# A twelve-layer perceiver kernel: batches of the head-wise cross attention reordered, one mask product in place of two, and layers begun on three quarters of their tokens

## The reference

```python
def cross(q_in, ctx, mask):                     # layer 4; layer 10 has no mask and one shared k and v head
    q, k, v = heads(q_in @ Wq + bq), heads(ctx @ Wk + bk), heads(ctx @ Wv + bv)
    s = where(mask, q @ k.T / sqrt(8), -1e9)    # 64 x 16 x 32 x 257
    return merge(softmax(s) @ v) @ Wo + bo
x = x + cross(layernorm(x), ctx, mask)
```

## Time and profile before

| | us |
|---|---|
| median of three runs | 3074.31 (3073.43 to 3076.48) |
| the profiled execution, own time | 3070.85 |
| its span | 3069.1 |
| mean granted TensorE clock | 0.95 of full |

### The profile page before, as it was taken

How to read it: one execution, slowest core, us unless ns; L and a number is a source line. 1 busy time by engine, 2 the same in 40 slices (tenths; PEclk the granted TensorE clock), 3 DMA queues, 4 the chain that set the end, 5 groups by cost and what they waited for, 6 DMA issues and landing times.

```text
span 3069.1 us, 71179 instructions
## 1 busy us (share of the span) xinstructions
PE 2812.5 (92%) x27569; PEld 1813.6 (59%) x27569; DVE 1702.2 (55%) x5653; ACT 1319.7 (43%) x3579; POOL 689.9 (22%) x1524
## 2 busy tenths in 40 slices
PE   8999998997999978999689997779999999999898
PEld 7888885554567755665457775534444444444465
DVE  6777777674166677558746765842233232232544
ACT  4655555542278842348538883411111121121222
POOL 2444440000067720024116661100000000000000
PEclk9999999998999988888779998989999999999999
DMA  5111110000021100230011113040000000000000
GB/s 133 49 47 47 49 31 8 2 3 5 12 55 48 48 25 3 67 106 2 5 40 43 39 29 142 2 136 1 1 1 1 1 1 1 1 1 1 1 1 14
DMA packets 125910, 92.28 MB, mean 30 GB/s; under 512 B 41027, under 2 KB 122566, under 8 KB 124230
## 3 DMA queue, kind: packets, MB, share of 16 engines
q1 hardware_dynamic: 125574, 87.74, 10.1%
HBM read 84.02 MB, written 3.67 MB: 29 GB/s over the span
## 4 chain that ended last, share of the span: by engine, by line
PE 54%; DVE 7%; issue 5%; POOL 4%; ACT 3%; DVEq 2%; POOLq 2%; ACTq 0%
PE banks L3349 24%; POOL probs L1208 3%; PE banks L918 2%; PE banks L3768 2%; PE banks L3759 2%; PE banks L3757 2%; PE banks L1682 2%; PE banks L899 1%; POOLq L1209 1%; PE banks L927 1%; PE banks L886 1%; PE banks L3404 1%; PE banks L2301 1%; PE banks L3359 1%; PE banks L1924 1%
## 5 line engine op out<-in xcount | busy, mean ns | idle before, releaser
L1008 ACT ACTIVATE probs<-probs,nbias 128x257 f32<-128x257 f32 x512 | 254.7, 507 | 0.0
L1208 POOL TENSOR_SCALAR probs<-probs,rinv 128x257 f32<-128x257 f32 x512 | 237.9, 485 | 29.3 <-DVE rinv L1102 25.6
L3349 PE MATMUL banks<-Wz,hT 128*64 128x256 f32 x2048 | 226.4, 379 | 0.0
L3349 PE MATMUL banks<-Wn,hT 128*64 128x512 f32 x1024 | 225.4, 593 | 0.0
L3349 PE MATMUL banks<-Wr,hT 128*64 128x512 f32 x1024 | 225.2, 592 | 0.0
L3618 POOL COPY rb<-hT 128x512 f32<-128x512 f32 x32 | 35.8, 1119 | 801.3 <-ACT hT L3424 777.0
L3349 PEld LDWEIGHTS banks<-Wz,hT 128*64 128x64 f32 x2048 | 147.0, 137 | 87.7 <-issue 18.3
L3592 DVE TENSOR_TENSOR pr<-hb,banks 128x512 f32<-128x512 f32 x32 | 22.0, 688 | 298.3 <-PE banks L3404 298.3
L712 POOL TENSOR_SCALAR probs<-probs,rinv 128x257 f32<-128x257 f32 x256 | 120.6, 485 | 201.3 <-DVE rinv L652 200.7
L3349 PEld LDWEIGHTS banks<-Wr,hT 128*64 128x64 f32 x1024 | 73.5, 137 | 132.6 <-issue 128.0
L3349 PEld LDWEIGHTS banks<-Wn,hT 128*64 128x64 f32 x1024 | 70.9, 137 | 129.5 <-issue 129.5
(11 more groups left out here) (632 smaller groups left out, 6399.2 us busy)
## 6 DMA issues: line engine op xcount, KB each, us to landing
kvT<-in_ctx_T SPq DMA_DIRECT2D x192, 128.5 KB
kv<-in_ctx SPq DMA_DIRECT2D x64, 128.0 KB
kv<-in_ctx SPq DMA_DIRECT2D x32, 256.0 KB
W<-in_L_ffn_W_T SPq DMA_DIRECT2D x2, 2048.0 KB
Wr<-in_L_ffn_w_hh_T SPq DMA_DIRECT2D x1, 4096.0 KB
Wn<-in_L_ffn_w_hh_T SPq DMA_DIRECT2D x1, 4096.0 KB
Wz<-in_L_ffn_w_hh_T SPq DMA_DIRECT2D x1, 4096.0 KB
v_last<-v_last SPq DMA_DIRECT2D x192, 8.0 KB, 1.6
```

The costliest lines, as they stand in the source:

```text
L1008: i = e.activation(s, s, ACT.Exp, bias=self.nbias[v][:, r:r + 1], scale=self.scale, accum_out=self.rows_sum[v][:, r:r + 1])
L1208: e.tensor_scalar(s, s, self.rinv[v][:, r:r + 1], 1.0, ALU.mult, ALU.mult)
L3349: mm = e.matmul(self.bank[b][hf * BATCH:(hf + 1) * BATCH, 0:n], lhs, rhs, start=start, stop=stop, tile_position=(0, hf * BATCH))
```

## The change

1. In layers 4 and 10 keys and values are made six batches ahead instead of five, on TensorE behind the scores instead of ahead of them, with a ring of seven value tiles instead of six. ScalarE makes the exponentials of g+3 ahead of the copies of keys and values. GpSimd's put_k_last moves along.
2. In layer 4 one product with the mask stays: it adds -BIG to masked scores (sink), and the row maxima's instruction multiplies by a factor (1 for seen places, a small number for masked ones that brings -BIG to the masked value) where it added a fill.
3. Nine layer starts (2, 3, 4 and 6 to 11) are reordered: norm_pe and norm_act_yT take a list of quarters, the layer's first products wait only for the quarters that they read, and quarter 3 is transposed a little later inside the layer. Where banks 0 to 3 are in use by then, the transposes go to others (TURN_BANKS). In layer 3 VectorE makes the signs ahead of the norm.

```diff
+    TURN_BANKS = (0, 1, 2, 3)
...
     def norm_dve(self, e):
-
-        quarters = range(3 if self.index else 0, 4)
+        self.norm_dve_statistics(e)
+        self.norm_dve_rows(e)
+
+    def own_quarters(self):
+        return range(3 if self.index else 0, 4)
+
+    def norm_dve_statistics(self, e):
         self.prog.x_loaded.wait_ge(e, 1)
-        for q in quarters:
+        for q in self.own_quarters():
...
-    X_BANK, T_BANK, AV, RING, PROBS, V_RING = 4, 5, 7, 4, 5, 6
+    X_BANK, T_BANK, AV, RING, PROBS, V_RING = 4, 5, 7, 4, 5, 7
...
-        p.constants_made.wait_ge(e, 1)
+        self.norm_pe(e, (0,))
...
+        self.norm_pe(e, (1, 2))
+        self.x_free = None
+        self.n_yT.wait_ge(e, 1)
+        self.prep_act.wait_ge(e, 1)
+        self.project(e, 0)
         self.prep_act.wait_ge(e, 3)
         e.matmul(bank[7][:, 0:P], p.ones[0:1, :], self.bo_eff[:, :], start=True, stop=True).then_inc(self.prep_mm.up(), 1)
-        self.norm_pe(e)
-        self.x_free = None
+        self.keys_values(e, 0)
+        self.norm_pe(e, (3,))
         self.n_yT.wait_ge(e, 4)
-        self.project(e, 0)
-        self.keys_values(e, 0)
         self.prep_act.wait_ge(e, 4)
         self.prep_pool.wait_ge(e, 1)
-        for g in range(1, 5):
+        for g in range(1, 6):
             self.keys_values(e, g)
+            if g == 5:
+                break
...
-            if g + 5 < BATCH:
-                self.keys_values(e, g + 5)
             if g + 4 < BATCH:
                 self.scores(e, g + 4)
+            if g + 6 < BATCH:
+                self.keys_values(e, g + 6)
             if b == 3 and t + 2 < NT:
                 self.project(e, t + 2)
             if b == 1 and t:
...
-            for n in range(2):
-                for r in range(4):
-                    rows = slice(32 * r, 32 * r + 32)
-                    i = e.matmul(self.bank[r][:, 0:CTX], self.tiled_ident[n][rows, :], self.lift[t % 2][rows, b * CTX:(b + 1) * CTX],
-                                 start=False, stop=n == 1)
-                    if n:
-                        i.then_inc(self.scored.up(), 1)
+            for r in range(4):
+                rows = slice(32 * r, 32 * r + 32)
+                e.matmul(self.bank[r][:, 0:CTX], self.tiled_ident[rows, :], self.sink[t % 2][rows, b * CTX:(b + 1) * CTX],
+                         start=False, stop=True).then_inc(self.scored.up(), 1)
...
+        self.copy_keys_values(e, 5)
         self.copy_pT1(e, 0)
         for g in range(BATCH):
-            if g + 5 < BATCH:
-                self.copy_keys_values(e, g + 5)
             if g + 3 < BATCH:
                 self.exponentials(e, g + 3)
+            if g + 6 < BATCH:
+                self.copy_keys_values(e, g + 6)
...
-        self.norm_dve(e)
+        self.norm_dve_statistics(e)
         self.weights_wait(e)
         self.take_queries(e, 0)
+        self.norm_dve_rows(e)
...
-            add = self.fill[t % 2][:, b * CTX:(b + 1) * CTX]
+            with_mask, op = self.factor[t % 2][:, b * CTX:(b + 1) * CTX], ALU.mult
         else:
-            add = self.zeros[:, :]
+            with_mask, op = self.zeros[:, :], ALU.add
...
-            i = e.tensor_tensor_reduce(self.probs[v][:, r * CTX:(r + 1) * CTX], self.bank[r][:, 0:CTX], add, 1.0, -3.0e38, ALU.add, ALU.max,
+            i = e.tensor_tensor_reduce(self.probs[v][:, r * CTX:(r + 1) * CTX], self.bank[r][:, 0:CTX], with_mask, 1.0, -3.0e38, op, ALU.max,
...
-        self.prog.rowed.wait_ge(e, NT * (self.index + 1))
-        self.map_lift(e, 0)
-        self.map_fill(e, 0)
+        self.map_sink(e, 0)
+        self.map_factor(e, 0)
...
-            if g + 5 < BATCH:
-                self.put_k_last(e, g + 5)
+            if g + 6 < BATCH:
+                self.put_k_last(e, g + 6)
...
-        e.tensor_scalar(self.lift[t % 2][:, :], self.mask_u8[:, :], -self.BIG, self.BIG, ALU.mult, ALU.add)
-
-    def map_fill(self, e, t):
+        e.tensor_scalar(self.sink[t % 2][:, :], self.mask_u8[:, :], self.BIG, -self.BIG, ALU.mult, ALU.add)
...
-        e.tensor_scalar(self.fill[t % 2][:, :], self.mask_u8[:, :], -to, to, ALU.mult, ALU.add)
+        e.tensor_scalar(self.factor[t % 2][:, :], self.mask_u8[:, :], 1.0 - f, f, ALU.mult, ALU.add)
...
-        self.norm_pe(e)
+        self.norm_pe(e, (0, 1, 2))
         self.weights_wait(e)
         for c in range(self.C):
             self.features(e, 0, c)
+            if c == 1:
+                self.norm_pe(e, (3,))
...
-            self.n_yT.wait_ge(e, 4)
+            self.n_yT.wait_ge(e, r + t + 1 if r == 0 else 4)
...
+        self.norm_act_yT(e, (0, 1))
         self.norm_act_std(e)
-        self.norm_act_yT(e)
+        self.norm_act_yT(e, (2,))
...
-        self.norm_pe(e)
+        self.norm_pe(e, (0, 1, 2))
...
+            if r == 2:
+                self.norm_pe(e, (3,))
             for c in range(FC):
+                self.n_yT.wait_ge(e, max(r, c % 2) + 1)
                 self.relu0.wait_ge(e, FC * r + c - 1)
...
+            self.signs_ready.wait_ge(e, 3)
+            self.n_yT.wait_ge(e, 3)
...
+        self.weights_wait(e)
         FC = self.FC
         for r in range(self.ROUNDS):
             h0, h1 = self.h[r % 2]
+            if r == 1:
+                self.norm_act_std(e)
+            if r == 2:
+                self.signs_ready.wait_ge(e, 3)
+                self.norm_act_yT(e, (3,))
             self.mm2.wait_ge(e, r - 1)
             for c in range(FC):
                 self.mm0.wait_ge(e, FC * r + c + 1)
...
                         self.next_root(e, q)
 
     def dve(self, e):
+        self.weights_wait(e)
+        e.tensor_scalar(self.W[0][:, :], self.raw[0][:, :], 2.0, -1.0, ALU.mult, ALU.add)
+        e.drain()
+        e.tensor_tensor(self.W[0][:, 0:512], self.W[0][:, 0:512], self.W[0][:, 512:1024], ALU.subtract).then_inc(self.signs_ready.up(), 1)
+        e.tensor_scalar(self.scales[:, 1:3], self.scales[:, 1:3], 2.0, None, ALU.mult).then_inc(self.signs_ready.up(), 1)
+        for n in range(1, 3):
+            e.tensor_scalar(self.W[n][:, :], self.raw[n][:, :], 2.0, -1.0, ALU.mult, ALU.add)
+        e.drain().then_inc(self.signs_ready.up(), 1)
         self.norm_dve(e)
-        self.weights_wait(e)
-        for n in range(3):
-            e.tensor_scalar(self.W[n][:, :], self.raw[n][:, :], 2.0, -1.0, ALU.mult, ALU.add)
-        e.tensor_scalar(self.scales[:, 1:3], self.scales[:, 1:3], 2.0, None, ALU.mult)
-        e.drain()
-        e.tensor_tensor(self.W[0][:, 0:512], self.W[0][:, 0:512], self.W[0][:, 512:1024], ALU.subtract)
-        e.drain().then_inc(self.signs_ready.up(), 1)
```

122 lines of the change are left out of this document (76 added, 46 removed).

## The result

The changed kernel takes 3195.81 us (median of four runs, 3189.34 to 3201.5); the kernel before, on the same chip, 3073.87. The ratio is 1.0398 with a 95% interval of 1.0374 to 1.0421: slower by 122 us. The forecast was 3197. The profiled execution took 3196.2 us, its span is 3194.5.

The account below looks back on a forecast made before the run. TensorE, busy 92% and without slack in layers 4 and 10, with ScalarE nearly full, was taken as the bound; 141 (loop) - 1 (mask product) - 17 (layer starts) = +123 us gave 3197 us, range 3155 to 3250.

Parts of the forecast that it names:

- The loop: Layers 4 and 10: TensorE's second user of bank 4 waits for ScalarE's delayed v copy; +141 us, bounds 122 to 170.
- The term for b = 0: In the round's iteration without a second user of bank 4, VectorE's late row maxima delay the next scores: +0.3 us.
- The upper bound of the loop: 85 us a layer in layers 4 and 10, with the raw 3.59 us and VectorE late in every iteration; 170 together.
- rival (d): Copies and stall are real, but TensorE catches up in b = 0 and layer starts gain their upper bound: 3160, chance 0.06.
- exponentials before the copies: Heading for layers 4 and 10: ScalarE's four exponentials now precede the kT and v copies; priced at +141 us together.
- TensorE has no slack: Layer 4's steady round: TensorE busy 15.43 of 15.48 us, so a new wait on it shows in the time at once.
- The mask product: Layer 4: four of eight bf16 matmuls per batch go, mostly hidden in waits; 1 us gained, bounds 0 and 4.
- The layer starts: Nine layers begin on three quarters: layer 2 gains 2.5 us, layer 3 3.5, others 11; 17 together, bounds 6 and 26.
- What would show it: Signs named: rounds of 20 to 21.5 us, 41 waits for v a layer of 1.3 to 1.9 us, clock near 1.00.
- (a): VectorE joins the loop in layers 4 and 10: exponentials wait 0.2 to 0.3 us more for nbias; 3225, chance 0.13.
- (b): TensorE's clock falls because it idles more, 7.4 us a round over half the 28 rounds: 3300, chance 0.09.
- (c): Faster: TensorE does not meet the wait for v, and rounds fall to about 14.4 us: 3026, chance 0.04.

Follow-up runs that it names:

- old-loops kernel: The changed kernel with both loop orders of layers 4 and 10 as before, five batches ahead; single mask product and new layer starts stay: 3056.74 us, ratio 0.9947.

## Why the prediction was right, and where it was not

**The loop (141 us).** Right in mechanism and size. From the start of one pT copy to the next, steady round of layer 4:

| iteration | before | forecast | measured |
|---|---|---|---|
| b = 0 | 3.3 | 3.6 | 3.81 |
| b = 1 | 3.54 | 5.25 | 5.22 |
| b = 2 | 4.66 | 6.3 | 6.22 |
| b = 3 | 3.96 | 5.5 | 5.47 |
| round | 15.48 | 20.7 | 20.72 |

Over the 64 batches, first pT copy to last, layer 4 took 238.8 us before and 310.1 now (+71.3; forecast 71), layer 10 234.8 and 303.8 (+69.0; forecast 70). The waits for v are 40 in layer 4 (41 named), in the weight loads 1.69, 1.28 and 1.25 us (1.3 to 1.9 named).

**The term for b = 0** was undersized, 0.3 for 0.5 us a round. The cause it names, VectorE's late row maxima, is what the rows show: the scores come 0.12 us behind the last maximum, while the spread queries had been ready for 0.36 us. In the sum that is 3 us a layer too little, and the terms for b = 1 to 3 a little too large make up for it.

**Readings.** The prediction takes the 0.24 us in the rows of the kernel before for a wait for v. The weight load behind the mask product comes 0.21 us late there also where it has nobody to wait for (L927 in b = 0), so only some 0.03 us of it was a wait for v, and L936's 0.31 us ends with GpSimd's p_last. The upper bound of the loop, 85 us a layer, does not hold both things that it names: with the raw 3.59 us (41 times 0.29 more) and VectorE late in every iteration (14 more) the sum is 97. And the 3160 of rival (d) has no working. None of these entered the forecast itself.

**What the sum left implicit.** It treats the 141 us as the price of "exponentials before the copies". The runs show that either order alone costs (scores first 109, exponentials first 161), so undoing the exponentials' edit gives back only 34 us. The sum was right because it followed all of TensorE's and ScalarE's order round the loop once; its heading, "exponentials before the copies", would have misled anyone who mended the kernel by it. Nor does "TensorE has no slack" say what bounded the kernel before: taking 0.3 us of TensorE's work out of a round left it at 15.47.

**The mask product** (1 us, 0 to 4): the round of the changed kernel shows 0.1, or 1.4 us in layer 4; the timed difference of 3 us has an interval wider than itself. The reason given, that it falls into the wait for ScalarE, is what the rows show (1.28 against 1.17).

**The layer starts** (17 us, 6 to 26) were oversized, and the two that the prediction works out, layers 2 and 3, both came out otherwise. The old-loops kernel has the starts and the mask product and is 16 us faster than before, where the sum has 18 for the two. The kernel with the mask product alone stands at 0.9976 against 0.9947, which leaves 9 us for the starts, give or take 6. The traces give another reading, since five of the profiled kernels have the old starts and eight the new. What lies outside the two loops (all of the span but first to last pT copy in layers 4 and 10) takes 2588.8 to 2600.1 us with the old starts and 2578.5 to 2587.9 with the new, 12 us less in the mean. By layer, in us (the first transpose is the first row of L240 or L246 in a layer):

| from, to | old starts, 5 profiles | new starts, 8 profiles | means |
|---|---|---|---|
| first transpose of 2, of 3 | 275.8 to 284.2 | 278.6 to 284.2 | +1.2 |
| first transpose of 3, first scores of 4 | 109.0 to 110.4 | 102.6 to 103.4 | -6.7 |
| first transpose of 6, of 7 | 103.5 to 107.3 | 102.3 to 107.0 | +0.3 |
| first transpose of 7, of 8 | 87.2 to 88.1 | 85.8 to 87.5 | -1.7 |
| first transpose of 8, of 9 | 143.9 to 145.5 | 138.8 to 142.8 | -3.9 |
| first transpose of 9, first pT copy of 10 | 111.3 to 116.0 | 112.7 to 114.4 | -0.6 |
| first transpose of 11, of 12 | 163.4 to 167.5 | 165.4 to 172.0 | +1.4 |

So the rows of layers 3 (with the start of 4), 7 and 8 give it all. In the working an earlier start is taken for a gain, and that step failed in layer 2. Its first product comes 2.9 us earlier in the profiled pair (2.5 forecast), but the layer as a whole shows no gain, within a spread of some 8 us between kernels in which it is the same. The rows at 466.88 and 468.21 show 0.60 us of transposes and a wait of 0.74 inside it. Layer 3 has its first product 3.7 us earlier (3.5 forecast), and with the start of layer 4 in the row the gain is 6.7; which of the two brings the rest is not shown. Under "What would show it" the prediction gives these gains, 2.5 and 3.5 us, as the distance from first transpose to first product; the distances are 1.48 and 2.61.

**The total.** In the profiled pair the loops grow by 140.3 us and all the rest shrinks by 15.0, which is the 125 us between the spans; by the medians it is 139 less 16. The forecast has 141 less 18. The loop term is right by its mechanism. That the rest came within 2 to 3 us is in part luck: no start that the prediction works out gave what it says, and over all profiles the starts are worth nearer 12 than 17.

**Rivals.** (a) no wait for nbias appears in the changed kernel; it does in the run with the exponentials first alone. (b) The clock stayed at 1.00 in the steady part. The Trainium skill, page Perfetto Trace Analysis, section Matmul Optimizations, says that the matmul engine scales its power with utilization (the prediction leaves out the word power); here 16.03 us busy of 20.72 (77%) kept the upper level, and about the same share (15.13 of 20 us) in the run with the exponentials first alone had 0.91. The share of busy time did not tell the two apart, and the measurement decides. The longest wait did differ (1.69 against 2.42 us), but no run shows that it is the cause. (c) and (d) did not come about: TensorE met the wait in every round, and b = 0 grew rather than shrank.

## What to carry to other kernels

When a PSUM bank has two users in a row, look at what stands ahead of its evacuation (the copy that empties it) on the evacuating engine: here, beyond 0.3 to 0.5 us of slack, every us put there became about a us of wait. Place the second user where the evacuation that it needs is an iteration old, and place independent work (here attend) between it and the next user, so that the third engine's take is covered too. And price a reordering round the whole loop, since two edits that each cost may be each other's cover: undo them one at a time before naming one as the cause.

## What the runs showed of the hardware

TensorE's granted clock fell again and again in the kernel with the exponentials alone moved, and not in the loops of the changed kernel, though both were busy 77% of the time. In layer 4 from 870 to 1170 us the first had 229.9 us busy at 0.98 and the second 232.3 at 1.00; in layer 10 the first had 223.7 of 290 us (1700 to 1990) at 0.95 and the second 231.7 of 299.4 (1670.6 to 1970) at 1.00. Busy time by stretch of the kernel with the exponentials alone moved, two stretches of layer 4:

```profile
980.00:1000.00 20.00, 14.85 (x215) 11.49 (x206) 10.67 (x47) 13.50 (x45) 12.59 (x31) 1.00 0.15 35
...
1060.00:1080.00 20.00, 15.13 (x212) 11.66 (x205) 9.93 (x50) 12.63 (x44) 10.48 (x25) 0.91 0.14 36
```

The one with more work had the lower clock. What TensorE had done before the fall at about 1063 us was to wait 1.61 us before L936 and 2.42 us before L947, and it had done the same in the round ahead (1.62 and 2.44) without a fall. What decides between them is open.

The other surprise: the weight load behind the mask product comes 0.32 us late whatever it is, with nobody to wait for (0.21 with two products). The matmuls are behind their weight loads there: with the load of L897 at 1047.88, PE rows run without a gap from 1047.12 to 1048.58 (their ends are modelled). So such a wait marked "issue" looks like backlog, and not like idle time that a reordering could win.
